# A decoder layer on one core: the order of VectorE and ScalarE work where one batch hands over to the next

## What is computed

```
x = x + window_attention(layernorm(x))       32 heads, 8 key heads, rope, causal window of 32 keys
x = x + cross_attention(layernorm(x), ctx)   16 heads, keys and values from a latent context
x = x + ffn(layernorm(x))

ffn:  h = silu(x @ w_gate) * (x @ w_up)      256 -> 1024
      in every group of 4 values of h, keep the 2 of largest magnitude, zero the others
      return h_sparse @ w_down               1024 -> 256
```

## Time and profile before

| | us |
|---|---|
| median of 3 runs | 424.14 (423.71 to 425.94) |
| the profiled execution | 424.8 |
| its span, first to last instruction | 423.0 |
| busy PE, share of the span | 398.2, 94% |
| busy DVE | 286.3, 68% |
| busy ACT | 206.1, 49% |
| busy POOL | 160.3, 38% |
| mean granted TensorE clock | 0.995 of full |

### The profile page before, as it was taken

One profiled execution on the slowest core, in us unless ns is written; L12 is line 12 of the kernel. 1 busy time (PEld: TensorE's weight loads), 2 busy tenths in 40 slices (PEclk: granted clock), 3 DMA queues, 4 the chain that ended last, 5 costly groups with the idle time before them and its releaser, 6 DMA issues.

```text
span 423.0 us, 8030 instructions
## 1 busy us (share of the span) xinstructions
PE 398.2 (94%) x2981; PEld 320.0 (76%) x2982; DVE 286.3 (68%) x610; ACT 206.1 (49%) x531; POOL 160.3 (38%) x160
## 2 busy tenths in 40 slices
PE   8998999899998899999999899999999898988996
PEld 8667778667697777777798777877789676756795
DVE  5977931779768971688858992678857992346263
ACT  1373731587335731487444642287444452188330
POOL 4552790388311420377510430167620340057000
PEclk9998999999999999999999999999999999999999
DMA  7975431312001200242001300242000400230000
GB/s 218 355 288 146 123 104 37 114 26 70 3 7 67 84 2 25 77 124 71 0 8 51 102 0 2 99 108 62 2 2 2 149 2 2 82 95 0 2 2 25
DMA packets 33447, 28.90 MB, mean 68 GB/s; under 512 B 18689, under 2 KB 28033, under 8 KB 33153
## 3 DMA queue, kind: packets, MB, share of 16 engines
q1 hardware_dynamic: 33408, 28.40, 21.4%
HBM read 19.21 MB, written 5.24 MB: 58 GB/s over the span
## 4 chain that ended last, share of the span: by engine, by line
PE 60%; DVE 18%; ACT 8%; issue 7%; POOL 4%; DMA 1%; SPq 1%; POOLq 0%; DVEq 0%; ACTq 0%
PE ps L569 13%; PE ps L442 11%; PE ps L633 7%; PE ps L512 7%; ACT prob L1178 4%; PE ps L533 3%; PE ps L451 3%; PE ps L555 3%; PE ps L649 3%; POOL prob L1071 2%; DVE mx L869 2%; DVE total L883 2%; DVE rope L841 2%; PE ps L608 2%; PE ps L494 2%
## 5 line engine op out<-in xcount | busy, mean ns | idle before, releaser
L1071 POOL TENSOR_TENSOR prob<-prob,inv 128x512 f32<-128x512 f32 x80 | 83.4, 1048 | 97.9 <-DVE inv L889 97.8
L442 PE MATMUL ps<-xnT,wqk_sb 128*128 128x256 f32 x320 | 77.9, 384 | 0.8 <-DVE rope L841 0.4
L442 PEld LDWEIGHTS ps<-xnT,wqk_sb 128*128 128x128 f32 x320 | 57.5, 190 | 12.2 <-issue 5.7
L1178 ACT ACTIVATE prob<-ps,mx 128x128 f32<-128x128 f32 (+1 forms) x128 | 53.1, 435 | 15.5 <-DVE mx L867 12.3
L1064 POOL TENSOR_TENSOR qs<-rope 128x512 f32<-128x512 f32 x32 | 40.8, 1274 | 43.4 <-DVE rope L841 40.7
L512 PE MATMUL ps<-ident_sb,prob 128*128 128x128 f32 x320 | 49.3, 278 | 7.5 <-POOL prob L1071 7.5
L1188 ACT ACTIVATE pT<-ps 128x512 f32<-128x512 f32 x80 | 48.0, 604 | 12.0 <-PE ps L512 11.7
L841 DVE TENSOR_TENSOR rope<-ps,trig_sb 64x512 f32<-64x512 f32 x74 | 50.9, 688 | 1.0
L512 PEld LDWEIGHTS ps<-ident_sb,prob 128*128 128x128 f32 x320 | 36.6, 140 | 16.4 <-POOL prob L1071 11.9
L867 DVE TENSOR_REDUCE mx<-ps 128x2 f32<-128x512 f32 (+1 forms) x48 | 32.7, 689 | 13.0 <-PE ps L494 12.4
L1050 POOL TENSOR_TENSOR rstd<-vareps,power 128x1 f32<-128x1 f32 x24 | 13.1, 550 | 73.8 <-DVE vareps L820 73.6
(11 more groups left out here) (123 smaller groups left out, 687.0 us busy)
## 6 DMA issues: line engine op xcount, KB each, us to landing
k<-kx SPq DMA_DIRECT2D x32, 128.0 KB, 2.9
q<-qx SPq DMA_DIRECT2D x32, 128.0 KB, 2.5
vb<-v_sb SPq DMA_DIRECT2D x42, 64.0 KB, 2.1
wqk_sb<-in_wqk SPq DMA_DIRECT2D x4, 512.0 KB, 7.5
work<-in_wgu SPq DMA_DIRECT2D x4, 512.0 KB, 8.8
wo_sb<-in_wo SPq DMA_DIRECT2D x1, 2048.0 KB, 14.5
vb<-v_sb SPq DMA_DIRECT2D x36, 32.0 KB, 2.2
wd_sb<-in_wd SPq DMA_DIRECT2D x1, 1024.0 KB, 5.8
```

The costliest lines, as they stand in the source:

```text
L442: mm = pe.matmul(o[:, half, :], wqk_sb[:, k, g, half, :], xnT[:, 0, k, :], start=(k == 0), stop=(k == KT - 1))
L1071: pool.tensor_tensor(p, p, inv[:, i % ND, 0:g].unsqueeze(2).broadcast_to([P, g, 512 // g]), ALU.mult).then_inc(s_norm, 1)
L1178: ins = act.activation(prob[:, i % ND, h * k:(h + 1) * k], ps[:, BANK_S + i % 2, h * k:(h + 1) * k], ACT.Exp, bias=mx[:, i % ND, h:h + 1], ...
```

## The change

Three things are moved; nothing is added or taken away. On DVE a new function `first_units` replaces the two places where the first units were written out: the second unit's maximum and subtraction now come before the sum of unit 0, and `keys_rest` comes behind that sum. In the handover the two `chunk_values` of the second chunk stand behind the maxima of units 0 and 1. `add_out("down")` goes from the end of the handover to behind all eight self units, between the statistics and the normalisation of the next rows (in the last sequence, which has none, directly in front of the sparsification). On ACT the two `magnitudes` of the second chunk go from in front of the first exponential into the next batch, behind `unit_out` of units 4 and 5. The last sequence's own second chunk keeps its place. At the very start `first_units(0, None)` is run too, so that `keys_rest` moves there as well.

```diff
@@ DVE
+            def first_units(b, prior):
+                unit_max(b, 0)
+                for i in range(1, HEAD):
+                    unit_max(b, i)
+                    if i == 1 and b:
+                        for j in range(2):
+                            chunk_values(b - 1, 1, j)
+                    unit_sum(b, i - 1)
+                    if i == 1:
+                        keys_rest(prior)
+
@@ DVE batch, behind the self units
                     for t in range(TT):
                         row_moments(rows[b + 1], 0, 3 * b + 2, t)
+                    if b:
+                        add_out("down", b - 1, b - 1)
                     for t in range(TT):
                         normalise(rows[b + 1], 0, 3 * b + 2, t, ("ln3", b - 1) if b else ("ln1", None))
+                elif b:
+                    add_out("down", b - 1, b - 1)
                 if b:
                     sparsify(b - 1, 1)
@@ DVE batch, the handover
                 sparsify(b, 0)
-                for j in range(2):
-                    chunk_values(b, 1, j)
-                if more:
-                    unit_max(b + 1, 0)
-                    keys_rest(b)
-                    for i in range(1, HEAD):
-                        unit_max(b + 1, i)
-                        unit_sum(b + 1, i - 1)
+                if not more:
+                    for j in range(2):
+                        chunk_values(b, 1, j)
+                if more:
+                    first_units(b + 1, b)
                 else:
                     sparsify(b, 1)
-                add_out("down", b, b)
+                    add_out("down", b, b)
@@ DVE, before the first batch
-            unit_max(0, 0)
-            keys_rest(None)
-            for i in range(1, HEAD):
-                unit_max(0, i)
-                unit_sum(0, i - 1)
+            first_units(0, None)
@@ ACT batch, self units
                     if i < NQB:
                         unit_exp(b, i)
+                    elif b and i < NQB + 2:
+                        magnitudes(b - 1, 1, i - NQB)
@@ ACT batch, the handover
                     for j in range(2):
                         gate(b, c, j)
-                    for j in range(2):
-                        magnitudes(b, c, j)
+                    if c == 0 or not more:
+                        for j in range(2):
+                            magnitudes(b, c, j)
```

## The result

| | before | after |
|---|---|---|
| median, us | 423.98 (423.63 to 426.07, 13 runs) | 420.59 (419.40 to 423.52, 13 runs) |
| ratio after to before | | 0.9925, 95% interval 0.9901 to 0.9949 |
| span of the profiled execution, us | 423.0 | 418.7 |
| busy PE, us | 398.2 | 396.8 |
| DVE, ACT, POOL busy, us | 286.3, 206.1, 160.3 | 285.2, 205.5, 160.0 |

The change makes the kernel 3.4 us faster, 0.75%. The forecast was 3.8 us.

The account below looks back on a forecast made before the run. DVE's chain was taken to set the end of the self units, with TensorE busy nearly all the time. Handovers -6.3, last-sequence stall +1.9 and start +0.6 gave -3.8 us: 420.3 us from 424.14, range 418.2 to 422.9.

Parts of the forecast that it names:

- The bound and the place: In the self units DVE's chain sets the end; ending them earlier is kept while PE has no gaps behind.
- The handovers: Between sequences, 1.80 us of wait and 0.56 of `add_out` leave DVE's chain: 2.1 us earlier at each of three, -6.3 us.
- the new wait: At each handover DVE's first maximum waits 0.3 us for scores of unit 0, which the products covered before.
- Sequences 1 and 2: Behind the self units, later magnitudes delay the sparsification, but normalised rows reach PE's `cross_norm` with 0.4 us to spare.
- The last sequence: Sparsification waits for the late magnitudes, so PE stalls 1.9 us at `cross_norm` for normalised rows, and nothing later absorbs it.
- The choice of 5.21 us: Length taken for the last sequence's sparsification, POOL being idle by then; with 6.33 us the stall would be 3.0 us.
- The clock: Rival: the last sequence's stall lowers TensorE's clock, 1.5 us for one short dip, 421.8 us; chance 0.14.
- signs of being wrong: PE waiting at L432 in sequences 1 and 2, clock under 1.00 behind 354 us, or a self-unit PE gap eating 2.1 us.
- The long dip: Rival: the clock stays low from `cross_norm` of sequence 3 for 12 us of PE work, +7.7, 428 us; chance 0.06.
- The start: At the very start `keys_rest` was free; moved behind sum 0 it adds 0.6 us to DVE's chain.
- The sum: Whole kernel: -6.3 + 1.9 + 0.6 = -3.8 us, to 420.3 us, 0.9% faster.
- The table rival: Magnitudes on ACT need another function table than the exponential: about 0.5 us in each of three sequences, 421.9 us; chance 0.04.

Follow-up runs that it names:

- mags_old: Changed kernel with the second chunk's magnitudes on ACT back in front of the first exponential, as in the kernel before; median 427.42 us, ratio 1.0069.
- mags_later: Changed kernel with the second chunk's two magnitudes one unit later still, behind the outputs of units 5 and 6; median 431.38 us, ratio 1.0170.
- keys_add_2: Second run of the kernel before with only `keys_rest` behind sum 0 at the handovers and `add_out` behind the self units; median 416.85 us, ratio 0.9840.
- mags_early: Changed kernel with the second chunk's two magnitudes on ACT at the handover, between the exponentials of units 1 and 2; median 418.64 us, ratio 0.9860.
- keys_only: Kernel before with only `keys_rest` moved behind sum 0 at the handovers; median 419.24 us, ratio 0.9893.
- filler_half: Changed kernel with four calls of unused matmuls on PE before the last sequence's second-half projection; median 420.62 us, ratio 0.9909.
- first set: First of three sets of experiments, each run beside executions of the kernel before; there the changed kernel ran again, at median 420.98 us.
- filler: Changed kernel with eight calls of unused matmuls on PE before the last sequence's second-half projection; median 420.80 us, ratio 0.9928.
- after_again: The changed kernel itself, run again without alteration beside the kernel before; median 420.98 us, ratio 0.9931.
- start_old: Changed kernel with the old order of the first units at the very start only, `keys_rest` directly behind maximum 0; median 420.73 us, ratio 0.9923.
- add_only: Kernel before with only the addition of the down product moved behind the self units; median 422.39 us, ratio 0.9986.

## Why the prediction was right, and where it wasn't

- **The bound and the place** were right: DVE's chain ends the self units, and behind them everything follows. All that shortened that chain shortened the distance between the sequences by as much, in every kernel of the table but the two that were made to stall (mags_old, mags_later).
- **The handovers**, -2.1 us each: -2.17, -2.14, -2.17. Its terms were 1.80 for the wait, 0.56 for the addition, against 0.3 for the new wait; alone they measured 1.77 to 1.83, 0.60 to 0.62, and 0.21 or 0.22 as the difference between keys_add_2 and mags_early.
- **What I left unasked** is whether all parts are needed. With the products in place and only `keys_rest` moved, the same layout puts the turn of sum 0 at 128.53 + 2 x 1.32 = 131.2, just when the old exponential 0 ended (129.29 + 1.28 + 0.63); I never laid that out, and it is keys_only. The two parts that are most of the change, products and magnitudes, bring nothing: they cost 0.2 us at each handover and the stall in the last sequence.
- **Sequences 1 and 2** hold, as forecast; DVE waits 2.54 us for the magnitudes there, for 2.6 laid out. To spare were 157.39 - 156.59 = 0.8 us at the bank and 159.12 - 158.53 = 0.6 us at the rows, for 0.4 laid out; the sparsification started 1.15 us behind the output, for the 1.23 I had taken, and lasted 5.14 us for 5.21.
- **The last sequence**: the price was right, 1.87 us for 1.9; what failed is the name of the first wait. I took `cross_norm` for the first reader of what DVE does late; it is the bank that the second half of the projection shares with the first. The sizes agree because the two readers lie so close: the rows are normalised 351.44 - 349.50 = 1.9 us after the bank is free, and PE has 1.7 us of work between the two. So at full clock most of the stall is taken at the bank, and the normalised rows, which I had laid out, still set its whole length, by 0.2 us (filler_half). That the sum came out without the bank in it is luck in how the two lie.
- **The choice of 5.21 us** over 6.33 for the sparsification was right: 5.14. The Trainium skill (SBUF — State Buffer, "SBUF: two separate sides") has VectorE and GpSimd take turns at a shared port pair, and this case's traces agree: next to POOL's norm one comparison took 1.52 us or 1.41 (mags_early), away from it 0.69.
- **The clock** as a rival had 0.14 for one dip. It came in the profiled execution, at 1.46 us for the 1.5 laid out, and a clock under 1.00 there was one of my signs of being wrong. The size agrees in part by luck: I had priced each microsecond of work at 0.6 to 0.7 more, from a score group of 1.71 us for 1.05, and here eight matmuls took 3.65 us for 1.89, so the dip held less work and cost more for each piece. Side by side in the first set, 11 of 12 executions of the changed kernel had a clock under 0.999, for 11 of 23 of the kernel before. That is the mis-sized chance: a rival with its condition in plain sight (PE busy 1.20 of 2.00 us, then 1.9 us of nothing) needed more than half. The wait isn't the only condition. Of the kept traces, the four with the late bank in the last sequence and no filler (after, after_again, start_old, mags_later) all have the fall behind it, the two with a filler don't, and of the six without the late bank three have it (add_only, keys_add_2, mags_old) and three don't (before, mags_early, keys_only). In mags_later the same wait of 2.00 us was followed by a clock of 0.55 and 0.60 (160 to 164 us) in sequence 1 and of 1.00 in sequence 2. The long dip, 428 us, came in neither trace of the changed kernel: the clock was back within 5 us. But one of its 25 executions took 427.7 us at 0.984, and eight had 0.988 to 0.992; none of these has a trace, so what happened in them stays open.
- **The start**, +0.6 us, is the term of the sum that failed. It was read from one trace in which the clock happened to be low, so that the scores of unit 1 came late enough for `keys_rest` to cost nothing: moving it costs 0.4 us then, 0 otherwise.
- **The sum** came close to the median (-3.8 for -3.4) by luck, because those two errors offset. At full clock the change is 423.8 - 419.5 = 4.3 us, which is the sum without the start, -4.4. In the median about 1 us of it goes back to the clock.
- **The table rival** fell: the counts of table loads are 4 for the gates and 3 for the exponentials, as before, with none at the magnitudes (one more, at the very start, is in both). The Trainium skill (ScalarE: Activation LUTs, "Table sets: the hidden batching unit") puts abs in every set, and the trace agrees.

## What to carry to other kernels

When a chain has a wait in it, look first for the one step that could fill it: one line moved (`keys_rest` behind the next maximum) brought more than the rearrangement around it. When work is put off into a stage with slack, list every reader of what is queued behind it, the PSUM banks that wait to be emptied among them, and look at the last round of the loop by itself, where the cover is gone. And price a wait of TensorE above its length: here 1.9 us of it were followed by another 1.2 to 1.5 us of clock in the three traces with that wait, though 5 of 25 executions ran at full clock all the same.

## What the runs showed of the hardware

- The granted clock at a place varies from one execution of the same program to the next. In the start of this kernel TensorE is busy about 1.6 of 2.00 us in the stretches 30 to 32 and 32 to 34 us of every trace (1.64 and 1.58 in most); in before, add_only and filler_half the clock then fell to 0.50, in after, keys_only and mags_early it stayed at 1.00.
- At the start a dip cost 0.8 us, in the scores which the first maximum waits for (1.87 us in before, 1.05 in after); behind that maximum it cost nothing with the old order, 16.5 us to the first projection either way. In the last sequence, where TensorE was the bound, it cost 1.2 to 1.6 us (17.22 for 15.99 in after_again, 15.72 for 14.12 in add_only, with no wait added).
- Eight unused matmul instructions in the place of 1.9 us of idle time kept the clock at 1.00 in one trace (filler_half), with TensorE busy for 1.19 and 1.29 of 2.00 us in the stretches 346 to 348 and 348 to 350 us; without them TensorE was busy for 0.67 and 0.45 of 2.00 us there, and the clock fell.
